# Sorted tokens in 512-row pages opened image by image; finished images turned and stored during the expert stage

## What is computed

```
x = x + attention(_ln_c(x))                       # per image, 1024 x 1024 scores per head
t = _to_tokens(x)                                 # (16, 1024, 192)
probs  = softmax(_ln_t(t) @ gate_w + gate_b)      # 4 experts
masked = probs * top2mask; masked /= sum + 1e-9
h = gelu(_ln_t(t) @ w1[e] + b1[e])                # 192 -> 768
y = h @ w2[e] + b2[e]                             # 768 -> 192
t = t + sum_e masked[e] * y[e]
x = _from_tokens(t, x)                            # back to (16, 192, 32, 32)
```

## Time and profile before

| | us |
|---|---|
| median of 3 runs | 2823.03 |
| the 3 runs | 2817.43 to 2830.2 |
| the profiled execution's own time | 2849.2 |
| its span | 2846.6 |
| setup, to TensorE's first job of the first image | 0 to 38.6 |
| attention | 38.6 to 1802.2 |
| expert stage | 1802.2 to 2770.2 |
| output stage | 2770.3 to 2846.6 |

### The profile page before, as it was taken

One profiled execution on the slowest core, in us unless ns is written; L12 is line 12 of the kernel. 1 busy time (PEld: TensorE's weight loads), 2 busy tenths in 40 slices (PEclk: granted clock), 3 DMA queues, 4 the chain that ended last, 5 costly groups with the idle time before them and its releaser, 6 DMA issues. The chain is left out here.

```text
span 2846.6 us, 58847 instructions
## 1 busy us (share of the span) xinstructions
PE 2505.1 (88%) x18693; PEld 1321.8 (46%) x18693; DVE 1710.0 (60%) x4886; ACT 1786.6 (63%) x2228; POOL 1406.2 (49%) x1136
## 2 busy tenths in 40 slices
PE   4699889889889888888888887599999999999975
PEld 2334333333333333333333322377777777777754
DVE  6557666666666666666666656555555555555522
ACT  2487677667667667667677675355556555655542
POOL 2334435435425434434434432477777777777750
PEclk9799999999999999999999999799999999999997
DMA  3211111111111111111111133444444444444419
GB/s 87 56 50 41 46 45 47 45 46 51 41 46 50 43 48 51 39 49 51 40 49 52 39 114 129 177 150 172 162 160 168 151 175 156 167 161 159 175 62 334
DMA packets 160274, 276.40 MB, mean 97 GB/s; under 512 B 21552, under 2 KB 129552, under 8 KB 150576
## 3 DMA queue, kind: packets, MB, share of 16 engines
q1 hardware_dynamic: 141648, 245.37, 26.8%
q0 software_dynamic: 13344, 27.87, 2.7%
q10 hardware_dynamic: 5056, 0.42, 0.3%
HBM read 174.07 MB, written 49.59 MB: 79 GB/s over the span
## 5 line engine op out<-in xcount | busy, mean ns | idle before, releaser
L784 ACT ACTIVATE probs<-ps_s 128x1024 f32<-128x1024 f32 x1024 | 1013.6, 1022 | 335.7 <-PE ps_s L683 329.5
L1351 POOL TENSOR_TENSOR h_split<-h_f,h_split 128x512 f16<-128x512 f32 x444 | 552.3, 1244 | 237.1 <-ACT h_f L1328 230.1
L696 PE MATMUL ps_o<-probs,v_aug 128*32 128x512 f32 x4096 | 573.6, 634 | 0.6 <-ACT probs L784 0.6
L1046 POOL TENSOR_TENSOR inv_norm<-sumsq,minus_half 128x16 f32<-128x16 f32 x128 | 375.2, 2932 | 401.1 <-DVE sumsq L989 400.8
L1278 PE MATMUL ps_h<-m_xn_t,packs 128*128 128x512 f16 x2220 | 552.6, 380 | 0.5 <-DVE m_xn_t L1413 0.5
L1324 ACT ACTIVATE h_split<-ps_h,packs 128x512 f16<-128x512 f32 x444 | 305.1, 687 | 391.5 <-PE ps_h L1278 391.5
L1292 PE MATMUL ps_y<-packs,h_split 128*128 128x192 f16 x5328 | 511.9, 245 | 0.8 <-POOL h_split L1351 0.8
L1292 PEld LDWEIGHTS ps_y<-packs,h_split 128*128 128x128 f16 x5328 | 452.9, 97 | 105.8 <-POOL h_split L1351 2.2
L683 PE MATMUL ps_s<-stacks_odd 98*128 98x512 f16 x1024 | 320.0, 399 | 27.1 <-DMA stacks_odd<-heads 23.3
L683 PE MATMUL ps_s<-even 98*128 98x512 f16 x1024 | 318.9, 397 | 22.8 <-DMA even<-heads 18.7
L1328 ACT ACTIVATE h_f<-ps_h,packs 128x512 f32<-128x512 f32 x444 | 301.7, 679 | 0.0
(11 more groups left out here) (213 smaller groups left out, 2883.0 us busy)
## 6 DMA issues: line engine op xcount, KB each, us to landing
packs<-expert_pack SPq DMA_DIRECT2D x74, 1635.0 KB, 6.9
even<-heads SPq DMA_DIRECT2D x192, 96.0 KB, 2.4
stacks_odd<-heads SPq DMA_DIRECT2D x192, 96.0 KB, 2.4
tile_rows<-sorted_rows SPq DMA_DIRECT2D x37, 400.0 KB, 6.6
tokens<-in_x_dram SPq DMA_DIRECT2D x17, 768.0 KB, 5.5
y_in<-y_tokens SPq DMA_DIRECT2D x16, 768.0 KB, 8.9
out_dram<-y_out SPq DMA_DIRECT2D x16, 768.0 KB, 7.1
even<-heads SPq DMA_DIRECT2D x128, 48.0 KB
```

The source lines that it names most:

```text
L696: mm = pe.matmul(ps_o[32 * j:32 * j + 32, f, :], v_aug[:, par, m, g * GH + j, :], probs[:, (GH * p + j) % PRING, f * HALF:(f + 1) * HALF], ...
L784: act.activation(probs[:, u % PRING, :], ps_s[:, u % 2, :, :].rearrange("p f n -> p (f n)"), ACT.Exp).then_inc(s_probs, 1)
L1046: pool.tensor_tensor(inv_norm[:, t, :], sumsq[:, t, :], minus_half[:, :], ALU.pow).then_inc(s_inv, 1)
L1351: pool.tensor_tensor(h_split[:, n % HSPLIT, 1, :], h_f32[:, n % HBUF, :], h_split[:, n % HSPLIT, 0, :], ALU.subtract).then_inc(s_h, 1)
```

## The change

**Pages.** `sorted_rows` has 37 x 512 rows in all. A pair's tokens fill 512-row pages; when an image brings a pair past a multiple of 512, new pages are opened behind all pages opened so far. All tokens of images 0 to b then lie in the first 2b+7 pages. Tile i is page i, so its start is a constant; its two experts stand in two new words of each row (`EXPERT`), and SP reads them from `sorted_rows` in DRAM instead of from the table in SBUF. Job z, `tile_table` and the table are gone.

**Routing.** Job r writes 18 columns instead of 6. The 6 instructions of VectorE become 25 (`row_places`), and `row_pairs` has 4 more, for each of the 16 images.

**Fill.** One transfer on ScalarE's queue writes all 37 pages (37 x 400 KB) in place of SP's 6.

**Finished images.** From tile 9 on, image b = 0 to 13 (`DONE_IMAGES` = 14) is turned in tiles 2b+9 and 2b+10: in steps 0 to 3 of each, TensorE turns one 128-token block (`turn_image`, 2 float32 transposes into the bank that `transposes` uses later in the tile), VectorE copies it to `y_half` (`take_image`). SP, in the middle of tile 2b+8, between the first and the second weight transfer, issues the store of image b-1 and the load of image b. The output stage is left with 2 images (`LEFT`).

```
-            sp.wait_ge(s_fill, 4)
-            for c in range(NPAIR):
-                sp.dma_start(mlp.rows[c * CAP:c * CAP + TROWS, :].rearrange("(p s) w -> p s w", s=SLOT),
-                             rows[:, 0:SLOT, :]).then_inc(s_filled, 16)
...
+            act.wait_ge(s_fill, 6)
+            act.dma_start(mlp.rows.rearrange("(i p s) w -> p i (s w)", p=P, s=SLOT),
+                          rows[:, 0:SLOT, :].rearrange("p s w -> p (s w)").unsqueeze(1).to_broadcast([P, NTILE, SLOT * ROW])
+                          ).then_inc(s_filled, 16)
...
-            route.now(dve.tensor_tensor(place[:, :], bank[:, 0:NPAIR], pair_base[:, :], ALU.add))
...
+            route.mark(dve.tensor_copy(place[:, :], bank[:, 0:NPAIR]))
+            dve.tensor_copy(held[:, :], bank[:, NPAIR:3 * NPAIR]).then_inc(s_job_done, 1)
             dve.wait_ge(s_job_done, done + 1)
...
+            row_places(dve, number, route)
...
     def load_rows(sp, i):
-        first = sp.value_load(mlp.table[0:1, 0, i:i + 1], min_val=0, max_val=NPAIR * CAP - TROWS)
         sp.dma_start(rows[:, i % 2, :, :],
-                     mlp.rows[bass.ds(first, TROWS), :].rearrange("(p s) w -> p s w", s=SLOT)).then_inc(s_row[i % 2], 16)
+                     mlp.rows[i * TROWS:(i + 1) * TROWS, :].rearrange("(p s) w -> p s w", s=SLOT)).then_inc(s_row[i % 2], 16)
...
+        named = mlp.rows[i * TROWS:i * TROWS + 1, EXPERT + slot:EXPERT + slot + 1].bitcast(I32)
+        e = sp.value_load(named, min_val=0, max_val=NE - 1)
...
+    def load_image(sp, b):
+
+        sp.wait_ge(s_put, 16 * SLOT * (2 * b + OUT_LAG - 1))
+        if b:
+            sp.wait_ge(s_t, NT * b)
+        sp.dma_start(y_back[:, :, :], y_img[b]).then_inc(s_in, 16)
+
+    def store_image(sp, b):
+        sp.wait_ge(s_t_done, NT * (b + 1))
+        sp.dma_start(out_img[b], y_half[:, :, :]).then_inc(s_out, 16)
+
+    def turn_image(pe, b, t):
+        if t == 0:
+            pe.wait_ge(s_in, 16 * (b + 1))
+        elif t != NT // 2:
+            pe.wait_ge(s_t_done, NT * b + t)
+        for k in range(2):
+            mm = pe.transpose(ps_j[0:HC, k * P:(k + 1) * P], y_back[:, t, k * HC:(k + 1) * HC], ident[:, :])
+        mm.then_inc(s_t, 1)
...
+            if done is not None and n < NT // 2:
+                turn_image(pe, done[0], done[1] + n)
...
                 for slot in range(2):
                     sp.wait_ge(s_w2, STEPS * i + NK * (slot + 1))
                     load_pack(sp, i + 2, slot)
+                    if slot == 0:
+                        images(sp, i)
```

More of the change, by code:

```diff
@@ L1295, in second_product, with transposes @@
         mm.then_inc(s_w2, 1)
-    def transposes(pe, tile, t):
+    def transposes(pe, tile, t, done):
         if t == 0:
             pe.wait_ge(s_xn, tile + 2)
+            if done is not None:
+                pe.wait_ge(s_t_done, NT * done[0] + done[1] + NT // 2)
         if not (isinstance(tile, int) and tile == -1 and t == 0):
@@ L1393, in dve_tile @@
                 add_expert(dve, tile, par, 0, own)
+            if done is not None and n < NT // 2:
+                take_image(dve, done[0], done[1] + n)
             if not has_next(tile):
```

210 lines of the change are left out of this document (113 added, 97 removed).

## The result

The changed kernel takes 2910.59 us (median of 4 runs, 2900.86 to 2921.45) where the kernel before takes 2826.61 (4 runs): the ratio is 1.0282, 95% interval [1.0255, 1.0308]. It is slower, by 84 us between the medians and by 80 by the ratio; the prediction was 2870, or 46.5 more, in a range of 2828 to 2912. The time lies 1.4 us inside the upper end of that range, and above the 2845 to 2895 to which the forecast gave its largest chance.

A forecast was written before the change was run, and what follows sets the result against it. The prediction took TensorE to bound the expert stage, job order and waits attention, transfers the output stage. Its terms, -57 + 13.5 + 13 + 10 + 2 + 25 + 40, gave +46.5, so 2870 us, range 2828 to 2912.

The forecast's parts named there:

- Output stage: End of the kernel: with 2 images left, the span ends 5.8 us after the second store, -57 us.
- Setup: Before TensorE's first job: the larger fill delays the start from 38.62 to near 52, +13.5 us, bounds 12 and 30.
- Routing, mid images: 13 images in mid-attention: the longer VectorE chain costs 1.0 us per image, bounds 0 and 4.4, +13 us.
- Routing, last three: Last three routings, where GpSimd waits for `index`: each 2.9 late, 0.7 more where `row_pairs` stands ahead, +10 us.
- Expert stage, start: First weight transfers wait for registers read from DRAM instead of SBUF: 1.4 us more taken, +2 us.
- Transposes and waits: Expert stage: 224 float32 transposes, +25 us; TensorE waiting 2.2 for the image in 13 images plus clock falls, +40 us.
- The base: The sum on the profiled span gives 2893; put on the runs' median of 2823.03 it gives 2870.
- The rival that came true: Rival 2: clock falls at unit 19 and at load waits, or setup goes to 30; each adds 15 to 40; chance 0.15.

The follow-up runs named there:

- second profile of before: The kernel before, unchanged, profiled once more: span 2827.4 against 2846.6 in the first profile, which the prediction used; timed 2828.15 us, ratio 0.9989.
- fill_sp: The changed kernel with its one large fill issued at the end of SP's setup queue instead of in ScalarE's: 2902.86 us, ratio 1.0255 to the kernel before.
- three: Changed kernel with image load and store ahead of weights, row places in pieces at units 13, 14, 16, fill behind bias issues: 2840.83 us, ratio 1.0036.
- no_turn: The changed kernel with all 16 images turned in the output stage, none in the expert stage: 2909.61 us, ratio 1.0291 to the kernel before.
- chain_before: The kernel before with 17 more dependent copies on VectorE behind place in all 16 routings: 2890.55 us, ratio 1.0204.
- load_early: The changed kernel with an image's load and the previous image's store issued ahead of the weights of slot 0: 2867.48 us, ratio 1.0134 to the kernel before.

## Why the prediction came out as it did

The side was right. The sum of +46.5 stands against +71.7 between the second profile of before and the profile after, +52.5 between the first one and that, and +84 between the medians. Term by term, from the table, against the second profile:

- **Output stage**: -57 predicted, 124.9 to 67.2 is -57.7. Right.
- **Setup**: +13.5 predicted, 22.5 measured. The failed step is "Nothing in the trace shows a queue refusing an issue behind full engines", from which the lower value was taken; with the changed kernel's fill one issue took 18.42 us, and the 18 us of bias issues came behind it. They were held until 38.27 and not, as the upper bound of 30 had it, until the fill had drained. fill_sp shows that this is not all of it: without the held queue the start is 59.05, because the biases' own transfers slow the fill. 38.7 returns only when the fill goes out last and nobody in the setup waits for it (three).
- **Routing, mid images**: +13 predicted, 34.4 in the 12 periods and 2.5 ahead of them, 37; in no_turn, with the same attention, 51. This is the term that made the prediction too low. Its working was right in each duration: 4.1 for the chain, 1.7 for GpSimd. The failed step is "I take 1.0, between these and below the 1.7", which counts on a half-clock stretch that "may go" and give back part of the wait. It did go, and against the first profile, from which it was read, an image pays 1.5 (17.6 in 12). But the second profile has no such stretch in 12 of 13 mid images, and the timed runs of before beside the experiments, at a mean clock of 0.956 to 0.962, are like the second (0.959) and not like the first (0.948). Against it there was nothing to give back: an image pays 2.9 for 3.0 (up to 4.3 in other profiles of the same routing code), and chain_before pays 3.7 for 3.9. Of the 2.9, 2.2 are in GpSimd's stretch from `inv_norm` to `inv_norm` (1.8 the wait for `index`, 0.3 a longer idle time ahead of its first issue), and 0.6 in units 0 to 7 (10.6 against 9.9), where TensorE's clock falls in all mid images and in the second profile in 7 of 13; what leads to that was not traced. The fault is less in the arithmetic than in one profiled execution being taken for the kernel.
- **Routing, last three**: +10 predicted, 193.8 to 203.9 is 10.1. There GpSimd's wait for `index` was already in the trace, and the same arithmetic, charged in full, was right in the sum; the three are 4.3, 2.0 and 3.8 (3.6, 2.9 and 3.6 predicted), and in other kernels with the same routing code the sum is 8.5 to 13.6.
- **Expert stage, start**: +2 predicted, -1 measured (20.9 to 19.9). A register read from DRAM takes 0.44 us in the median of 74, not 1.4 more than the read from SBUF (the first four, which this term is about, 0.46 to 2.19).
- **Transposes and waits**: 25 and 40 predicted, together 65; 60.9 measured. Of the 36 tiles 27 have an image's half in them, 27 x 0.87 is 23.5 (the 28th is in the last column of the table), the 13 waits are 27.7 (13 x 2.1, predicted 2.2), and 9.7 is left, 7.5 of it (4 x 1.9) the clock's falls (predicted 12 in all). That the wait came out so close is luck in part: in the third image the weights went out 1.4 behind the sixth product where 2.15 was put (0.75 and 1.4 for the read), and from there to the load's landing it was 11.5 where 10.9 was put (8.8, 1.2 and a 0.9 for completion that no row shows). load_early shows that the waits and the clock behind them are one cause, the order in SP's queue. The four passes of the Trainium skill (FP8 and Floating Point Precision, section TensorE Precision Notes), by which the term would have been 48, are not seen in these transposes: 8 of them between float16 matmuls add 0.87.
- **The base**: the sum was put on the median by taking the profiled execution's span for the kernel's. That execution's periods were 1.4 us longer each than in the second profile, which hid 17 us of what routing costs from a comparison of the first profiles, but not from the timed runs.

The rival that came true is the second, in an unforeseen part of it: the setup in the middle between its value and its upper bound, and the routing at three times its price, while the waits for images came out as forecast.

Not settled: the setup of unchanged code ends at 61.15 to 65.46 in different kernels' profiles although the last bias issue is out at 58.8 to 59.8 in all of them; and every second period is up to 7 us longer than its neighbours, with a mean clock down to 0.94 in one of 112.6 us, by an amount that differs between runs of the same attention code. Either may be part of the 10 us by which the median of the changed kernel lies above its profiled execution; no run tells.

## What to carry to other kernels

A chain of small dependent instructions is priced by asking for whom its engine works next, not by the share of busy time: VectorE was at 68% over the image, and a chain of 2.9 us on it cost 2.9, most of it because an engine behind it (GpSimd) worked back to back for 23 us from that point. Moving the chain one unit earlier, or in pieces with the scatter one unit later, was worse than leaving it; what helped, by 20 us, was to move other work of VectorE into its idle time ahead of that stretch (units 8 and 12).
A wait or a clock stretch that a prediction leans on is looked for in a second profiled execution first: the one here stood in all mid images of one profile and in one image of the other.
In a queue with three large transfers the one that is waited for goes first, if what it needs is there: 40 us for four moved lines.
A large fill that nobody needs for 100 us is issued last, with the wait at its first reader.

## What the runs showed of the hardware

- An issue in ScalarE's queue behind one transfer of 14,800 KB took 18.42 us, and the next five 1.0 each (4.96 in all) instead of 0.64.
- TensorE's wait of 2.68 us in a stage at full clock was followed by 6 us at a mean of 0.72; four tiles of thirteen show such a loss, behind waits of 2.17, 2.18, 2.43 and 2.68 us, nine show none, behind waits of 1.78 to 2.32. No rule is drawn from it here.
- In attention TensorE's wait at one point of each mid image was 2.3 us in one profile of the kernel before, with a granted clock of 0.94 over units 16 to 31, and 1.3 in the other, with 1.00; in the kernel three a wait of 4.25 was followed by 7 us at 0.61.
- A fill at 408 GB/s beside the first images' work cost them at most 1.5 us.
